# Mamba + SwiGLU layer on one core: du times B for two channel blocks per GpSimd instruction

## The chip, the cores and the metric

One core of one Trainium2 chip runs the whole program. The metric is the device time of one execution in microseconds. The kernel before takes 1815.21 us as the median of three runs (1815.02 to 1816.69).

## The reference, cut to what matters

Four sequences of 2048 tokens with 256 features go through a Mamba block, a layer norm, a SwiGLU feed-forward block with integer weights, and a second layer norm. The part that matters here:

```python
x_in, res = jnp.split(x @ W_in, 2, axis=-1)
x_conv = silu(_causal_dw_conv(x_in, conv_w, conv_b))          # u, 512 channels
dt, Bm, Cm = jnp.split(x_conv @ W_x, [DT_RANK, DT_RANK + N_STATE], axis=-1)
delta = softplus(dt @ W_dt + b_dt)
# per token, for 16 states of each channel
h = exp(delta * A) * h + delta * Bm * x_conv
y = einsum('bdn,bn->bd', h, Cm)
out = (y + x_conv * D) * silu(res) @ W_out
# feed-forward, weights are int32 times 1/127
h2 = silu(x1 @ wg.T) * (x1 @ wu.T);  out2 = h2 @ wd.T
```

## The kernel before, in words

The 8192 tokens are cut into 16 chunks of 512. Channels lie on the 128 partitions in four blocks (m = 0 to 3). One step of the program handles one chunk, in 64 beats: beat = 4n + m is state n of channel block m. In each beat

- ScalarE makes the exponential exp(delta times A) of the block (`exp`, L1104), normally into one of two PSUM banks, so that it waits for the scan two beats back;
- GpSimd makes du times B (`times_b`, L1247): du is delta times u of the block, B one row of the input spread over all partitions (`brep`). The result goes into one of DBU = 4 buffers in SBUF, so that the product of beat b waits for the scan of beat b - 4;
- VectorE scans along the 512 tokens (`scan`, L1429): it takes the exponential and the product, and writes h.

Then TensorE turns the states of each n so that tokens lie on partitions (`turn`, L747). The tokens of the upper half are weighted by C on ScalarE (`weigh`, L1113, tile gt) and turned back and summed by TensorE (`turn_back`, L772). Those of the lower half are summed on VectorE (`sum_states`, L1442, tile acc). State n is first turned at beat 4n + 4, and its weights and sums come at beats 4n + 5 and 4n + 7.

Everything else is threaded into the same beats by hand: the tables `FILL_AT` (the beat of each TensorE job of the next chunk's front and the last chunk's back: projections, convolution, feed-forward), `READ_AT` (when ScalarE or VectorE read the result) and `BEAT` (all other work). Each engine's queue is in program order: a wait holds up whatever is behind it.

Silu needs another activation table on ScalarE than exp. Two sessions in a step hold it, from beat 31 to 32.5 (silu of the next chunk's u and of this chunk's z) and from 43.5 to 45 (silu of the gate; in step 0, of z). Before a session's table load ScalarE makes the exponentials of the next AHEAD = 2 beats (32, 33 and 44, 45) into the SBUF tile `da_ahead`; the exponential of the beat behind them (34, 46) follows the table load that ends the session (L1189). Scans 32, 33, 44 and 45 so read both inputs from SBUF. `HOLD = (0, 3)` makes the product of beat 47 wait until scan 45 has ended.

GpSimd's other work: delta and du of the next chunk (`positive_part`, L1279, at beats 52, 55, 60, 63; `times_u`, L1286, at 53, 56, 63, 63), y times silu(z) (`times_z`, L1298, at 8, 11, 13, 17), the normalisation (L1271) and, in step 0 from beat 13, nine instructions that turn the integer weights into floats (`cast`, L1256, L1260).

In step 0 the first delta and du are VectorE's: `first_u(m)` (L1500 for delta, L1504 for du). Its place in the queue of VectorE is one beat ahead of need:

```python
for beat in range(NH):
    if first and beat + 1 < DB:
        first_u(beat + 1)
    scan(i, beat)
```

so the order is first_u(0), first_u(1), scan 0, first_u(2), scan 1, first_u(3), scan 2, scan 3. The tap buffer `xs` (128 partitions, 4 rows of 512) is filled by DMA from beat 56.5 on for the convolution of the chunk after next and last read by TensorE at beat 26.

Of the kernel before, what the change touches and what calls it, by code (L numbers as in the profile page):

```python
# [65 lines left out]
BEAT = {"soft exp": [48.5, 51, 56.5, 56.5], "soft ln": [49, 51.5, 57, 59.5], "add u": [52, 55, 60, 63],  # L66
        "times u": [53, 56, 63, 63], "x1 cut": [29, 35], "x1 low": [30.5, 31.5], "y upper": [5.5, 6.5],
        "times z": [8, 11, 13, 17], "mean": [21, 64], "rstd": [22, 79], "shift": [24, 90],
        "square": [(21, 21, 21, 21), (64, 65, 67, 76)], "norm": [(25, 26, 26, 26), (94, 100, 104, 104)],
        "halo": -23.5, "silu uz": [31, 32.5], "silu gate": [43.5, 45]}  # L70
# [81 lines left out]
def mamba_swiglu(nc, x, x_t, w_in, conv_w, conv_b, w_x, w_dt, b_dt, a_log, d_skip, w_out, w_gate_t, w_up_t,  # L152
# [31 lines left out]
    with ExitStack() as ctx:  # L184
# [153 lines left out]
        def ahead(beat):  # L338

            for start in SILUS:  # L340
                if start < beat <= start + AHEAD:
                    return beat - start - 1
            return None

# [176 lines left out]
        def _(pe):  # L521

            def taken(c, name):

                kind, n = name.rstrip("0123456789"), int(name[-1]) if name[-1].isdigit() else 0
                return {"xin": (xin_ready, c * (DB + 1) + n + 2), "conv": (conv_raw, c * DB + n + 1),
                        "res": (res_raw, (c - 1) * DB + n + 1), "dtb": (xd_ready, 2 * c + 2), "ct": (ct_ready, c + 1),
                        "dt": (dt_abs, c * DB + n + 1), "yt": (lower_copied, c * DP + n + 1),
                        "o": (res1_done, c * TT + n + 1), "x1t": (low_ready, c * KK + n + 1),
                        "gate": (gate_raw, c * HB + n + 1), "up": (hid_ready, c * HB + n + 1),  # L530
                        "down": (res2_done, (c + 1) * TT + n + 1), "first": (first_res_raw, n + 1)}[kind]


            held_before, last_in = {}, {}
            for i in range(NCH):
                for beat in range(NH):
                    for name in FILLS:
                        begun = [("first%d" % FIRST_RES.index(name), 0, FILL_AT[name])] if i == 0 and name in FIRST_RES else []
                        if name in F_FILLS:
                            begun += [(name, c, [at + NH * (c - i - 1) for at in fill_at(c, name)])  # L540
                                      for c in (i + 1, i + 2) if c < NCH]
                        elif i > 0:
                            begun.append((name, i - 1, FILL_AT[name]))
# [1053 lines left out]
```

## Time and profile before

| | |
|---|---|
| median of three runs | 1815.21 us |
| profiled execution, its own time | 1816.19 us |
| its span in the profile | 1814.4 us |
| granted TensorE clock, mean | 0.994 |
| TensorE matmul busy | 1688.8 us (93%) |
| VectorE busy | 1687.7 us (93%) |
| ScalarE busy | 1610.2 us (89%) |
| GpSimd busy | 1589.4 us (88%) |
| chain that ended last | TensorE 68%, ScalarE 20%, GpSimd 5%, issue 4%, VectorE 2% |

The span is the time from the first to the last instruction of the program; 1.8 us of the profiled execution's time lie around it, and its time is 1.0 us above the median. The starts of the 16 steps (scan of beat 0) lie 108.1 to 108.8 us apart. "Beat" below counts within a step; times are from the start of the span.

### The profile page before, as it was taken

To read this page: it belongs to the slowest core of one execution; us is meant where nothing else is said; L and a number is where in the kernel's file an instruction comes from. 1 tells how busy PE (TensorE), PEld (TensorE's weight loads), DVE (VectorE), ACT (ScalarE), POOL (GpSimd) and SP (SyncE) were. 2 spreads that over 40 slices of the span, in tenths; PEclk is the share of its full clock that TensorE was granted. 3 is DMA by queue.
4 is the path that set the end of the run, shared out by engine and by line. 5 is a ranking of instruction groups with operands and counts; after the bars stand their busy time and mean duration, and the time that the engine had idled before them with its cause. 6 is when DMAs were issued, how large, how long until landed. Compare 5 with 4: busy or idle time off the path is not lost.

```text
span 1814.4 us, 32052 instructions
## 1 busy us (share of the span) xinstructions
PE 1688.8 (93%) x10128; PEld 1267.4 (70%) x10128; DVE 1687.7 (93%) x1957; ACT 1610.2 (89%) x2769; POOL 1589.4 (88%) x1373
## 2 busy tenths in 40 slices
PE   8879899999999999899999999999899999998788
PEld 3556676776767677676776867677676776767677
DVE  4999999999999999999999999999999999999994
ACT  4898989899899998989899898998989899898874
POOL 2989799898989989899898989989899898989960
PEclk9999999999999999999999999999999999999999
DMA  7323123222222323223232222323223232221110
GB/s 242 117 71 117 48 83 117 71 108 80 105 83 82 109 91 117 71 82 117 71 116 72 105 89 77 116 85 115 71 82 117 71 117 71 106 84 46 40 42 25
DMA packets 82104, 164.53 MB, mean 91 GB/s; under 512 B 10369, under 2 KB 28033, under 8 KB 81938
## 3 DMA queue, kind: packets, MB, share of 16 engines
q1 hardware_dynamic: 80498, 160.90, 25.3%
q8 instruction: 85, 1.39, 0.3%
q10 hardware_dynamic: 1440, 1.58, 0.3%
q14 instruction: 81, 0.66, 0.1%
HBM read 87.47 MB, written 8.91 MB: 53 GB/s over the span
## 4 chain that ended last, share of the span: by engine, by line
PE 68%; ACT 20%; POOL 5%; issue 4%; DVE 2%; DMA 0%; DVEq 0%; SPq 0%; ACTq 0%; POOLq 0%
PE ht_upper L747 10%; PE ht_lower L747 10%; PE y_upper L772 9%; PE fill L569 8%; PE fill L683 8%; PE fill L673 6%; PE fill L652 5%; POOL dbu L1247 4%; PE fill L584 3%; ACT gt L1113 3%; ACT da L1104 3%; ACT L1189 2%; ACT L1177 2%; ACT da_ahead L1104 2%; PE fill L622 2%
## 5 line engine op out<-in xcount | busy, mean ns | idle before, releaser
L1247 POOL TENSOR_TENSOR dbu<-du,brep 128x512 f32<-128x512 f32 x1024 | 1296.4, 1298 | 157.0 <-DVE h L1429 132.2
L1429 DVE TENSOR_TENSOR_SCAN h<-da,h,dbu 128x512 f32<-128x512 f32 x720 | 888.8, 1269 | 35.4 <-ACT da L1104 32.9
L1104 ACT ACTIVATE da<-delta,a_s 128x512 f32<-128x512 f32 x960 | 659.9, 694 | 58.6 <-DVE h L1429 55.1
L1113 ACT ACTIVATE gt<-ht_upper,ct 128x512 f32<-128x512 f32 x512 | 351.1, 686 | 74.1 <-PE ht_upper L747 69.5
L747 PE MATMUL ht_upper<-ident,h 128*128 128x128 f32 x2048 | 314.1, 276 | 71.2 <-ACT gt L1113 53.5
L747 PEld LDWEIGHTS ht_upper<-ident,h 128*128 128x128 f32 x2048 | 242.9, 142 | 196.6 <-issue 126.8
L1442 DVE SCALAR_TENSOR_TENSOR acc<-ht_lower,ct,acc 128x512 f32<-128x512 f32 x480 | 350.7, 731 | 7.5 <-PE ht_lower L747 6.1
L747 PE MATMUL ht_lower<-ident,h 128*128 128x128 f32 x2048 | 313.1, 276 | 23.6 <-DVE acc L1442 19.7
L747 PEld LDWEIGHTS ht_lower<-ident,h 128*128 128x128 f32 x2048 | 240.2, 142 | 99.5 <-DVE h L1429 48.3
L772 PE MATMUL y_upper<-ident,gt 128*128 128x128 f32 x2048 | 308.7, 273 | 0.0
L1429 DVE TENSOR_TENSOR_SCAN h<-da,dbu 128x512 f32<-128x512 f32 x240 | 282.5, 1209 | 18.8 <-ACT da L1104 18.0
L772 PEld LDWEIGHTS y_upper<-ident,gt 128*128 128x128 f32 x2048 | 245.7, 142 | 43.4 <-issue 30.8
L569 PE MATMUL fill<-xt_s,win_s 128*128 128x512 f32 x456 | 224.6, 595 | 9.7 <-DVE x1t L1360 9.7
L683 PE MATMUL fill<-wd_s,kb 128*128 128x256 f32 x720 | 177.7, 380 | 0.0
L683 PEld LDWEIGHTS fill<-wd_s,kb 128*128 128x128 f32 x720 | 127.3, 190 | 17.8 <-issue 6.2
L652 PE MATMUL fill<-wout_s,kb 128*128 128x256 f32 x480 | 117.5, 383 | 0.3 <-ACT kb L930 0.3
L673 PE MATMUL fill<-x1t,wu_s 128*128 128x512 f32 x360 | 110.8, 428 | 1.5 <-DVE kb L1349 1.5
L673 PE MATMUL fill<-x1t,wg_s 128*128 128x512 f32 x360 | 107.3, 420 | 0.0
L569 PEld LDWEIGHTS fill<-xt_s,win_s 128*128 128x128 f32 x456 | 75.6, 190 | 43.3 <-issue 41.3
L652 PEld LDWEIGHTS fill<-wout_s,kb 128*128 128x128 f32 x480 | 84.9, 190 | 21.2 <-POOL kb L1298 10.9
L1298 POOL TENSOR_TENSOR kb<-kb,z 128x512 f32<-128x512 f32 x60 | 77.7, 1295 | 0.0
L1279 POOL TENSOR_TENSOR delta<-delta,du 128x512 f32<-128x512 f32 x60 | 76.7, 1278 | 0.2
(188 smaller groups left out, 1892.5 us busy)
## 6 DMA issues: line engine op xcount, KB each, us to landing
brep<-b_rows SPq DMA_DIRECT2D x127, 512.0 KB, 3.7
xs<-xin SPq DMA_DIRECT2D x242, 256.0 KB, 2.5
xr<-x SPq DMA_DIRECT2D x16, 512.0 KB, 3.9
xt_s<-x_t SPq DMA_DIRECT2D x15, 512.0 KB, 3.8
out<-xr SPq DMA_DIRECT2D x15, 512.0 KB, 2.8
win_s<-w_in SPq DMA_DIRECT2D x2, 512.0 KB, 5.3
h<-xin SPq DMA_DIRECT2D x4, 256.0 KB, 4.1
h<-xin ACTq DMA_DIRECT2D x4, 256.0 KB, 4.6
```

What stands on the lines that cost most here:

```text
L569: mm = nc.tensor.matmul(front_bank(c, name)[:, :], win_s[:, k, m * P:(m + 1) * P], xt_place(c)[:, k, :], start=(k == 0), stop=(k == KK - 1))
L652: mm = nc.tensor.matmul(fill_bank(name)[:, 0:DM], kb[:, m, t * P:(t + 1) * P], wout_s[:, m, :], start=(m == 0), stop=(m == DB - 1))
L673: mm = nc.tensor.matmul(fill_bank(name)[:, :], w[:, k, n * P:(n + 1) * P], x1t[:, half, k, :], start=(k == 0 and half == 0), stop=(k == KK ...
L683: mm = nc.tensor.matmul(fill_bank(name)[:, 0:DM], kb[:, n, t * P:(t + 1) * P], wd_s[:, n, :], start=(n == 0), stop=(n == HB - 1))
L747: mm = nc.tensor.transpose(bank[:, m * P:(m + 1) * P], h_times(i, n, m, t * P, (t + 1) * P), ident[:, :])
L772: mm = nc.tensor.matmul(y_upper[m // 2][:, (m % 2) * HALF + k * P:(m % 2) * HALF + (k + 1) * P], lhsT=gt[:, (n * UPPER + k) % GT, m * P:(m ...
L1104: nc.scalar.activation(dst[:, :], delta[:, par, m, :], ACT.Exp, scale=a_s[:, m, n:n + 1])\
L1113: nc.scalar.activation(gt[:, (n * UPPER + k) % GT, :], ht_upper[:, :], ACT.Copy, scale=ct[:, par, k, n:n + 1])\
L1247: nc.gpsimd.tensor_tensor(dbu[:, beat % DBU, :], du[:, par, m, :], brep[:, n // PIECE % 2, n % PIECE, :], ALU.mult).then_inc(dbu_ready, 1)
L1298: nc.gpsimd.tensor_tensor(kb[:, blocks, times], kb[:, blocks, times], z[:, par, blocks, times], ALU.mult)\
L1429: nc.vector.tensor_tensor_scan(h_times(i, n, m, 0, T), da[beat % 2][:, :] if slot is None else da_ahead[:, slot, :], dbu[:, beat % DBU, :] ...
L1442: nc.vector.scalar_tensor_tensor(out=acc[:, par, k, :], in0=ht_lower[:, :], scalar=ct[:, par, UPPER + k, n:n + 1], in1=acc[:, par, k, :], ...
```

## The change

GpSimd's product takes two channel blocks (beats b and b + 1, b even) in one instruction of 128 x 1024, with B read twice through a broadcast operand; it waits for both blocks' du and for the scans that free both buffers, and counts up by two when it ends. There are six product buffers. `da_ahead` is gone: the exponentials ahead (beats 32, 33, 44, 45) go to two rows of the tap buffer `xs`, with the waits which that needs on ScalarE and on the DMA queue of SyncE. Silu of z is two instructions of two blocks each, both at beat 32.5, in step 0 too. The nine weight casts are ScalarE's, at beats 12, 13, 14, 15, 18, 19, 36, 38, 40 of step 0. The tables `FILL_AT`, `BANK`, `READ_AT`, `EARLY_FILL` and `EARLY_READ` are written in another layout with the same values.

```diff
-CAST_AT, WEIGHT_PARTS = 13, 9
+CAST_AT = (12, 13, 14, 15, 18, 19, 36, 38, 40)
+WEIGHT_PARTS = len(CAST_AT)
-AHEAD = 2
-DBU = 4
+AHEAD = (('xs0', 'xs1'), ('xs0', 'xs1'))
+DBU = 6
 HOLD = (0, 3)
-        da_ahead = sb("da_ahead", [P, AHEAD, T])
...
             def shift_xin(c, m):
+                if m == 0 and c > 1 and LAST_XS is not None:
+                    sp.wait_ge(h_ready, (c - 2) * NH + LAST_XS + 1)
...
-            def silu_z(c, par):
-                act.wait_ge(res_raw, c * DB)
-                nc.scalar.activation(z[:, par, :, :], z[:, par, :, :], ACT.Silu).then_inc(z_ready, 1)
+            def silu_z(c, par, half):
+                blocks = slice(half * DP, (half + 1) * DP)
+                if c:
+                    act.wait_ge(res_raw, (c - 1) * DB + (half + 1) * DP)
+                else:
+                    act.wait_ge(first_res_raw, (half + 1) * DP)
+                nc.scalar.activation(z[:, par, blocks, :], z[:, par, blocks, :], ACT.Silu).then_inc(z_ready, 1)
...
+            def cast(n, k):
+                if n < 2:
+                    third = slice(k * (HID // 3), (k + 1) * (HID // 3))
+                    copy((wg_s, wu_s)[n][:, :, third], integers(n)[:, :, third].bitcast(I32)).then_inc(w_ready, 1)
+                else:
+                    third = slice(2 * k, 2 * k + 2)
+                    nc.scalar.activation(wd_s[:, third, :], wd_s[:, third, :].bitcast(I32), ACT.Copy, scale=W_SCALE)\
+                        .then_inc(w_ready, 1)
...
             def times_b(i, par, beat):
                 n, m = beat // DB, beat % DB
                 if n == 0:
-                    pool.wait_ge(du_ready, i * DB + m + 1)
+                    pool.wait_ge(du_ready, i * DB + m + 2)
...
-                used = beat - DBU if beat >= DBU else max(b for b in range(NH) if b % DBU == beat) - NH
-                after(pool, h_ready, i * NH + max(used, HELD.get(beat, used)) + 1)
-                nc.gpsimd.tensor_tensor(dbu[:, beat % DBU, :], du[:, par, m, :],
-                                        brep[:, n // PIECE % 2, n % PIECE, :], ALU.mult).then_inc(dbu_ready, 1)
+                for b in (beat, beat + 1):
+                    used = b - DBU if b >= DBU else max(other for other in range(NH) if other % DBU == b % DBU) - NH
+                    after(pool, h_ready, i * NH + max(used, HELD.get(b, used)) + 1)
+                nc.gpsimd.tensor_tensor(dbu[:, beat % DBU:beat % DBU + 2, :], du[:, par, m:m + 2, :],
+                                        brep[:, n // PIECE % 2, n % PIECE:n % PIECE + 1, :].broadcast_to([P, 2, T]),
+                                        ALU.mult).then_inc(dbu_ready, 2)
...
                 for beat in range(NH):
-                    times_b(i, par, beat)
+                    if beat % 2 == 0:
+                        times_b(i, par, beat)
```

With `HELD` = {47: 45}, the product of beats 46 and 47 waits for scan 45.

## Rows read from the trace of the kernel before

**Rows 1.** Busy time by engine, step 0 and step 8: stretch, us, busy of each engine
```profile
34.00:143.00 109.00, 85.77 (x483) 56.41 (x483) 97.67 (x97) 91.68 (x145) 98.29 (x82) 0.95 0.28 99
903.00:1012.00 109.00, 104.31 (x630) 78.45 (x630) 102.64 (x120) 100.74 (x176) 100.33 (x87) 1.00 0.27 93
```

**Rows 2.** Who waited for whom, whole span: us in total, times, longest
```profile
DVE h L1429 <- POOL dbu L1247: 0.3, 1, 0.3
```

**Rows 3.** Chain that ended last, step 8, silu of z: start, us, what
```profile
955.60 1.80 ACT z L998
```

**Rows 4.** Instruction groups: durations in ns (min/median/max, or mean behind the busy time)
```profile
L1247 POOL TENSOR_TENSOR dbu<-du,brep x1024: 1254/1282/2175, 32.1 to 1764.4; 128x512 f32<-128x512 f32 x171
...
L1266 POOL TENSOR_TENSOR stats<-stats 128x4 f32<-128x4 f32 x30 | 6.2, 205 | 23.9 <-ACT stats L1024 23.9
...
L1003 ACT ACTIVATE kb<-kb 128x1536 f32<-128x1536 f32 x30 | 44.4, 1482 | 0.2
...
L998 ACT ACTIVATE z<-z 128x2048 f32<-128x2048 f32 x16 | 30.6, 1914 | 0.0
```

**Rows 5.** Timeline, start of step 0, VectorE and GpSimd: start, us, what [idle before]
```profile
30.67 0.69 DVE L1504 TENSOR_TENSOR du<-delta,u 128x512 f32<-128x512 f32 x1
...
32.59 1.34 DVE L1504 TENSOR_TENSOR du<-delta,u 128x512 f32<-128x512 f32 x1
33.86 1.21 DVE L1429 TENSOR_TENSOR_SCAN h<-da,dbu 128x512 f32<-128x512 f32 x1
...
36.29 1.21 DVE L1429 TENSOR_TENSOR_SCAN h<-da,dbu 128x512 f32<-128x512 f32 x1
...
40.26 2.45 DVE L1429 TENSOR_TENSOR_SCAN h<-da,dbu 128x512 f32<-128x512 f32 x2 [0.31 <-POOL dbu L1247]
...
38.89 9.87 POOL L1247 TENSOR_TENSOR dbu<-du,brep 128x512 f32<-128x512 f32 x8 [1.17 <-DVE du L1504]
```

**Rows 6.** Chain that ended last, step 0, first turn of state 0
```profile
41.68 0.97 PE ht_upper L747 x4
```

**Rows 7.** Busy time by engine around it; the clock behind the last count
```profile
38.00:42.00 4.00, 4.00 (x6) 1.54 (x7) 3.66 (x5) 1.95 (x4) 3.11 (x3) 0.50 0.71 264
```

**Rows 8.** Timeline, step 8, scans 31 to 35, and GpSimd's products 31 to 35
```profile
951.38 1.21 DVE L1429 TENSOR_TENSOR_SCAN h<-da,dbu 128x512 f32<-128x512 f32 x1
...
953.76 3.24 DVE L1429 TENSOR_TENSOR_SCAN h<-da_ahead,dbu 128x512 f32<-128x512 f32 x2
...
959.44 2.41 DVE L1429 TENSOR_TENSOR_SCAN h<-da,dbu 128x512 f32<-128x512 f32 x2 [1.80 <-ACT da L1104]
...
948.60 6.19 POOL L1247 TENSOR_TENSOR dbu<-du,brep 128x512 f32<-128x512 f32 x5
```

**Rows 9.** Timeline, step 0, scans 32 to 34, products 32 to 35, exponential 34
```profile
86.69 5.23 DVE L1429 TENSOR_TENSOR_SCAN h<-da_ahead,dbu 128x512 f32<-128x512 f32 x2
...
92.48 1.21 DVE L1429 TENSOR_TENSOR_SCAN h<-da,dbu 128x512 f32<-128x512 f32 x1
...
84.74 4.99 POOL L1247 TENSOR_TENSOR dbu<-du,brep 128x512 f32<-128x512 f32 x4
...
90.60 0.69 ACT L1104 ACTIVATE da<-delta,a_s 128x512 f32<-128x512 f32 x1
```

**Rows 10.** Timeline, steps 0, 8: products from beat 47, scans of beats 46 and 64
```profile
109.32 6.34 POOL L1247 TENSOR_TENSOR dbu<-du,brep 128x512 f32<-128x512 f32 x5 [2.74 <-DVE h L1429]
...
111.86 2.41 DVE L1429 TENSOR_TENSOR_SCAN h<-da,dbu 128x512 f32<-128x512 f32 x2 [1.97 <-ACT da L1104]
...
142.66 2.51 DVE L1429 TENSOR_TENSOR_SCAN h<-da,h,dbu 128x512 f32<-128x512 f32 x2 [1.76 <-issue]
...
977.00 3.80 POOL L1247 TENSOR_TENSOR dbu<-du,brep 128x512 f32<-128x512 f32 x3 [2.79 <-DVE h L1429]
...
980.46 2.41 DVE L1429 TENSOR_TENSOR_SCAN h<-da,dbu 128x512 f32<-128x512 f32 x2
...
1011.61 2.45 DVE L1429 TENSOR_TENSOR_SCAN h<-da,h,dbu 128x512 f32<-128x512 f32 x2
```

More of the change, by code:

```diff
@@ L23 @@
 SILU_SET = "silu_and_others"
-FILL_AT = {"xin2": (2, 2), "xin3": (5, 7), "yt0": (6,), "yt1": (9,), "conv0": (10,), "o0": (10, 10, 13, 13),
[8 rows of a table removed]
+FILL_AT = {'xin2': (2, 2),
+ 'xin3': (5, 7),
+ 'yt0': (6,),
+ 'yt1': (9,),
+ 'conv0': (10,),
+ 'o0': (10, 10, 13, 13),
+ 'o1': (13, 13, 14, 14),
+ 'conv1': (14,),
+ 'o2': (17, 17, 17, 18),
+ 'o3': (18, 18, 18, 18),
+ 'conv2': (19,),
+ 'res0': (20, 20),
+ 'res1': (23, 24),
+ 'x1t0': (26,),
+ 'conv3': (26,),
+ 'x1t1': (28,),
+ 'res2': (31, 31),
+ 'gate0': (32, 35),
+ 'res3': (32, 33),
+ 'gate1': (35, 35),
+ 'gate2': (36, 37),
+ 'gate3': (38, 38),
+ 'gate4': (38, 38),
+ 'gate5': (39, 39),
+ 'up0': (40, 44),
+ 'dtb': (42, 42, 43, 43),
+ 'up1': (45, 45),
+ 'up2': (45, 45),
+ 'dt0': (45,),
+ 'ct': (45,),
+ 'up3': (47, 47),
+ 'up4': (48, 48),
+ 'dt1': (49,),
+ 'up5': (49, 49),
+ 'dt2': (50,),
+ 'dt3': (51,),
+ 'down0': (53, 53, 53, 53, 53, 54),
+ 'xin0': (-9, -9),
+ 'down1': (55, 56, 57, 57, 58, 58),
+ 'down2': (57, 59, 59, 59, 59, 60),
+ 'down3': (62, 62, 62, 62, 62, 62),
+ 'xin1': (-1, 0)}
 FILLS = list(FILL_AT)
 FRONT = ("xin", "conv", "res", "dtb", "ct", "dt")
-BANK = {"xin2": 1, "xin3": 0, "yt0": 1, "yt1": 1, "conv0": 0, "o0": 1, "o1": 0, "conv1": 1, "o2": 1, "o3": 0,
[4 rows of a table removed]
+BANK = {'xin2': 1,
+ 'xin3': 0,
+ 'yt0': 1,
+ 'yt1': 1,
+ 'conv0': 0,
+ 'o0': 1,
+ 'o1': 0,
+ 'conv1': 1,
+ 'o2': 1,
+ 'o3': 0,
+ 'conv2': 0,
+ 'res0': 1,
+ 'res1': 0,
+ 'x1t0': 1,
+ 'conv3': 0,
+ 'x1t1': 0,
+ 'res2': 1,
+ 'gate0': 0,
+ 'res3': 1,
+ 'gate1': 1,
+ 'gate2': 0,
+ 'gate3': 1,
+ 'gate4': 0,
+ 'gate5': 1,
+ 'up0': 1,
+ 'dtb': 0,
+ 'up1': 0,
+ 'up2': 1,
+ 'dt0': 0,
+ 'ct': 1,
+ 'up3': 1,
+ 'up4': 0,
+ 'dt1': 1,
+ 'up5': 0,
+ 'dt2': 1,
+ 'dt3': 0,
+ 'down0': 1,
+ 'xin0': 0,
+ 'down1': 1,
+ 'down2': 0,
+ 'down3': 1,
+ 'xin1': 0}
 F_FILLS = sorted((name for name in FILLS if name.rstrip("0123456789") in FRONT), key=lambda name: FILL_AT[name][-1])
@@ L57 @@
 GT = 4
-READ_AT = {"xin0": -6.5, "conv0": 13.5, "res0": 25, "xin1": 2, "conv1": 16, "res1": 26, "xin2": 4.5, "conv2": 23,
[5 rows of a table removed]
[L66 to L70, printed above, removed]
+READ_AT = {'xin0': -6.5,
+ 'conv0': 13.5,
+ 'res0': 25,
+ 'xin1': 2,
+ 'conv1': 16,
+ 'res1': 26,
+ 'xin2': 4.5,
+ 'conv2': 23,
+ 'res2': 32.5,
+ 'xin3': 9,
+ 'conv3': 28.5,
+ 'res3': 35,
+ 'dtb': 45,
+ 'ct': 47,
+ 'dt0': 48.5,
+ 'dt1': 50.5,
+ 'dt2': 52,
+ 'dt3': 54,
+ 'yt0': 8,
+ 'yt1': 10,
+ 'o0': 13.5,
+ 'o1': 14.5,
+ 'o2': 19,
+ 'o3': 19,
+ 'x1t0': 27.5,
+ 'x1t1': 29.5,
+ 'gate0': 36,
+ 'up0': 45.5,
+ 'gate1': 37,
+ 'up1': 45.5,
+ 'gate2': 38.5,
+ 'up2': 45.5,
+ 'gate3': 39.5,
+ 'up3': 48,
+ 'gate4': 40,
+ 'up4': 48,
+ 'gate5': 41,
+ 'up5': 50,
+ 'down0': 54,
+ 'down1': 59.5,
+ 'down2': 61.5,
+ 'down3': 63}
+BEAT = {'soft exp': [48.5, 51, 56.5, 56.5],
+ 'soft ln': [49, 51.5, 57, 59.5],
+ 'add u': [52, 55, 60, 63],
+ 'times u': [53, 56, 63, 63],
+ 'x1 cut': [29, 35],
+ 'x1 low': [30.5, 31.5],
+ 'y upper': [5.5, 6.5],
+ 'times z': [8, 11, 13, 17],
+ 'mean': [21, 64],
+ 'rstd': [22, 79],
+ 'shift': [24, 90],
+ 'square': [(21, 21, 21, 21), (64, 65, 67, 76)],
+ 'norm': [(25, 26, 26, 26), (94, 100, 104, 104)],
+ 'halo': -23.5,
+ 'silu a': [31, 32.5],
+ 'silu b': [43.5, 45],
+ 'silu at': [31, 32.5, 32.5, 43.5, 45]}
 FIRST_FILLS = ["xin0", "xin1", "xin2", "xin3", "conv2", "conv0", "conv1", "conv3", "dtb", "dt0", "dt1", "ct", "dt2", "dt3"]
@@ L336, in filled, with taken @@
             return signal, (c - (kind == "res")) * len(order) + order.index(name) + 1
[L338 to L343, printed above, removed]
+        def taken(c, name):
+            kind, n = name.rstrip("0123456789"), int(name[-1]) if name[-1].isdigit() else 0
+            return {"xin": (xin_ready, c * (DB + 1) + n + 2), "conv": (conv_raw, c * DB + n + 1),
+                    "res": (res_raw, (c - 1) * DB + n + 1), "dtb": (xd_ready, 2 * c + 2), "ct": (ct_ready, c + 1),
+                    "dt": (dt_abs, c * DB + n + 1), "yt": (lower_copied, c * DP + n + 1),
+                    "o": (res1_done, c * TT + n + 1), "x1t": (low_ready, c * KK + n + 1),
+                    "gate": (gate_raw, c * HB + n + 1), "up": (hid_ready, c * HB + n + 1),
+                    "down": (res2_done, (c + 1) * TT + n + 1), "first": (first_res_raw, n + 1),
+                    "da": (h_ready, c + 1)}[kind]
@@ L521, in _ @@
         def _(pe):
[L523 to L543, printed above, removed]
-                        for fill_name, c, beats in begun:
-                            if beats[0] == beat:
-                                place = BANK[name]
-                                held_before[c, fill_name] = last_in.get(place)
-                                last_in[place] = c, fill_name
             def wait_bank(c, name):
@@ L1194, in step @@
                 for beat in range(NH):
-                    if ahead(beat) is None and beat not in AFTER_SILU and not (first and beat < 2):
+                    if beat not in PLACES and beat not in AFTER_SILU and not (first and beat < 2):
                         exp(i, par, beat)
```

133 lines of the change are left out of this document (81 added, 52 removed), and 17 rows, old and new, of tables (BANK, FILL_AT, READ_AT).

## The prediction

> **What bounds the kernel now.** I read three things: busy time by step, then who waits for whom, then the chain that ended last. In a middle step all four engines are busy for 100 to 104 of 109 us [rows 1], so a busy share decides nothing. The waits say more: VectorE waited for GpSimd's product once, for 0.3 us [rows 2]. In the chain of a middle step TensorE runs without a break but for the first silu session, where ScalarE leads: silu of z, table load, exponential, weight, and only then the next turn of TensorE [rows 3]. So a middle step is TensorE's time plus ScalarE's session. GpSimd is hidden there. In step 0 it is otherwise: TensorE has 86 us of work in 109, VectorE and GpSimd 98 each [rows 1]. All that starts the pipeline lies there, and step 0 is the place to look at.
>
> **Price of a pair.** A product of 512 takes 1.28 us (median), the same operation on 4 elements 0.205 [rows 4]; that is 2.12 ns an element and 2.37 us for 1024. Eight in a row took 9.87 us [rows 5], that is (9.87 - 1.28) / 7 = 1.23 from start to start, 0.05 less than one lasts. So a pair takes 2.32 us of GpSimd's time if the fixed part is saved, 2.46 (two spacings) if it is not. I take 2.33, since one slope fits both rows. GpSimd saves some 32 x 0.13 = 4 us of work a step. As nobody waits for it, that brings nothing in a middle step.
>
> **Are the products still in time?** The tight place is the end of a step. In step 8 product 47 starts at 977.00, when scan 45 ends. Now the pair 46/47 starts there, because of the hold. Up to the pair of the next beats 0 and 1 GpSimd has ten pairs and eight delta and du operations of 1.23: 33.1 us (34.4 at 2.46), with no gate that closes in between, as six buffers let it run. It ends at 1010.1 to 1011.4, and scan 0 is at 1011.61 [rows 10]. In time, by 0.2 us at worst. Scan 46 is no trouble in a middle step: the pair is done at 979.3 to 979.5, and the scan comes at 980.46 [rows 10].
>
> **Start of step 0: +3.9 us.** Here the pair waits for two du, and VectorE makes them one beat ahead. Product 0 ran beside du(1), which took 1.34 us for that instead of 0.69 [rows 5]. Now du(1) ends at 32.59 + 0.69 = 33.28, the pair runs from 33.36 to 35.7, and scan 0 starts at 35.75 instead of 33.86. Scan 1 follows by the old spacing, 2.43 later, at 38.2. Behind it stands first_u(3), done after one more spacing, at 40.7. Only then may pair 2/3 start, and scan 2, next in VectorE's queue, waits for all of it, till 43.1; what is queued behind it waits too. Scan 3 follows at 44.3 instead of 40.26, and ends 4.0 later than before. TensorE's first turn began at 41.68, right behind scan 3's old end at 41.5 [rows 5, 6], and waits till 45.6: +3.9. Bounds: 3.0, if the pair were 0.5 shorter, and 4.4.
>
> **Clock of TensorE: +1.0.** Around 38 to 42 us the granted clock is 0.50, that is 1.2 GHz, after TensorE had idled for about 4 us [rows 7]. The new wait is another 3.9 us. The old stretch at half rate reached 2 us beyond the turn and cost 1 us; if the clock stays down for 4 to 5 us of the new work it costs 2.4. I take 1.0 more, bounds 0 and 2.4.
>
> From there the chain goes through TensorE's queue, nearly closed up to beat 20, and then through VectorE, so I let both terms through whole.
>
> **First session of step 0: +0.8.** Scans 32 and 33 take both inputs from SBUF, and then VectorE and GpSimd shut each other out: the two scans took 5.23 us, as the first waited for product 35 to end [rows 9]. It lost 2.9 us. With six buffers the pair 36/37 may start when scan 31 ends (one sum of VectorE, 0.6 us, before 86.69) and lasts till 88.5; the scan waits for it and ends at 89.6, not 90.8. That relief of 1.2 us would be worth having, but silu of z now stands in the first silu session of step 0 too: 1.91 us and 0.1 for the split (below) put exponential 34 from 90.60 to 92.5, and scan 34 from 92.48 to 93.2 or 93.3 [rows 9]. So +0.8, bounds 0.6 and 1.2. In the second session ScalarE gets the 1.9 us back, but scan 46 now waits for the held pair: 109.32 + 2.33 = 111.65, about where it was, 111.86 [rows 10].
>
> **End of step 0: -0.3.** Before, GpSimd led here: scan 0 of step 1 started at 142.66, after 1.76 us of idling. Ten pairs and eight others from 109.32 give 142.5 [rows 10] (143.8 at 2.46). Take -0.3; bounds -0.3 and +1.1.
>
> **Silu of z in two: +1.5.** 2048 elements take 1.914 us and 1536 take 1.482 [rows 4]: 0.84 ns an element, 0.19 fixed. A half takes 1.05, and since 1.91 us of it are 1.80 in the chain [rows 3], each further instruction costs about 0.1. It stands on the chain in the 15 steps after step 0. Bounds 0.05 and 0.2 each.
>
> **At nothing.** Casts: nine copies of 512 elements, by the same fit 0.62 us each, 5.6 in all; ScalarE idles 17 us of step 0 [rows 1], mostly waiting for TensorE and the scans at beats 12 to 40; if that cover went, up to 5.6. On GpSimd they are gone from a place where VectorE was full. Exponentials in `xs`: the same SBUF writes; the wait for conv3 (filled at beat 26, read at 28.5) is over by beat 31, and SyncE's wait for scan 45 is over by 56.5, where the tap DMA is issued, with stores and B loads behind it. Six buffers: no time of their own.
>
> **The port in the middle steps: 0.** Scan 32 starts at 953.76 and ended 2.1 us later. Scan 31 ends at 952.59; the pair 36/37 runs from then or from the end of 34/35 (952.5 to 953.3) to 955.0 or 955.8, so scan 33 ends at 957.3 to 958.0, and the sum behind it is done by 958.7. Scan 34 comes at 959.44, on ScalarE's time, after 1.80 us of idling [rows 8]: covered. In step 0 the waiting scan let products 34 and 35 pass, though they started after it [rows 9]; if the normalisation behind 36/37 passes too, 0.5 more, still covered. The Trainium skill (SBUF — State Buffer, Who interferes with whom) says that whoever issues first has the shared pair for the whole instruction and the other blocks. By that rule the scan of step 0 would have waited only for product 33; the trace disagrees. By the rule the middle steps end at 958.7, by the row at 959.2, and the sum is the same.
>
> **Sum.** 3.9 + 1.0 + 0.8 - 0.3 + 1.5 = +6.9. The profiled execution took 1816.2 (span 1814.4 and 1.8 around it), 1.0 above the median; 1823.1 against it, **1822.1** as a median. Its bounds: 3.0 + 0 + 0.6 - 0.3 + 0.8 = 4.1 and 4.4 + 2.4 + 1.2 + 1.1 + 3 = 12.1, so 1819.3 to 1827.3. A measurement can tell some 0.2%, 3.6 us, from no change, so slower begins at 1818.8 and faster below 1811.6.
>
> **Rivals.**
> - *The port is not covered* (0.13). The block doubles with the instruction. If scan 34 comes later than ScalarE's exponential by 0.5 to 1 us in 15 steps, +7.5 to 15 on top: 1830 to 1837. For it: only 0.2 to 0.7 us are left over. Against: the idle 1.80 us.
> - *The broadcast operand costs* (0.05). A pair of 2.6 us overruns the margin at scan 0 by some 0.7 us in each step (from six pairs between beats 54 and 0, and nine before): +11, so 1833.
> - *The late start is absorbed* (0.15). VectorE and ScalarE have small gaps between beats 4 and 20; if TensorE catches up there, both first terms go: 1817.2, no change by the measurement. Against: TensorE's queue is nearly closed there.
> - *Faster: GpSimd does pace* (0.09). The chain puts 5% of the span on GpSimd, 90 us, in step 0, at the end of step 14 and in step 15, where the scans and the products wait for each other in a ring. If those are its pace, the pairs save 0.13 in 2.46 of that, 4.8 us; with the 1.2 us of scan 32, the start absorbed and z at +0.8, -5.2: 1810.0. It decides wherever a scan waits for a product. Against: only 0.3 us of such waits [rows 2].
>
> **Numbers.** Forecast 0.58. Slower 0.58 + 0.13 + 0.05 = 0.76, same 0.15, faster 0.09. The range 1816.5 to 1831 takes in the forecast, the absorbed start and the lower edge of the port rival, and leaves out the faster case, the broadcast case and the rest of the port's.
>
> **What would show it.** Scan 2 of step 0 at 43.1 and TensorE's first turn at about 45.6; the clock at 0.50 once more behind it; product instructions of 2.37 us; scan 34 of step 0 at the exponential's end; step 1 starting about 5.4 us later than 142.66, at 148.1; the other steps 108.8, each 0.1 longer. Steps of 109.2 or more would speak for the port or the broadcast, steps under 108.6 for a GpSimd that paces. Step 1 starting before 145 would be the absorbed start.

## The result and the profile after

The changed kernel takes **1822.81 us** as the median of five runs (1822.15 to 1824.02), the kernel before 1815.21: a ratio of 1.0041, 95% interval 1.003 to 1.0052. It is slower by 0.4%: by 7.6 us in the medians and by 5.96 in the two profiled executions (1822.15 against 1816.19).

The page of the changed kernel, its span, busy time and the shares of the chain that ended last:

```profile
span 1820.3 us, 32112 instructions
...
PE 1691.9 (93%) x10128; PEld 1267.5 (70%) x10128; DVE 1695.2 (93%) x1957; ACT 1616.0 (89%) x2794; POOL 1517.8 (83%) x852
...
PE 71%; ACT 19%; issue 5%; DVE 4%; POOL 2%; DMA 0%; DVEq 0%; ACTq 0%; POOLq 0%; SPq 0%
```

GpSimd, at 88% before, is at 83%, and its share of the chain went from 5% to 2%: the work was saved, and the time did not follow. Who waited for whom in the changed kernel, total us, times, longest:

```profile
POOL dbu L1403 <- DVE h L1571: 174.8, 82, 7.0
...
POOL dbu L1403 <- DVE du L1645: 26.3, 2, 21.1
...
DVE h L1571 <- POOL dbu L1403: 5.2, 2, 2.6
```

Two waits of 2.6 us stand where 0.3 stood [rows 2]. Both lie at the start of step 0. VectorE there, then GpSimd (start, us, what, idle before); they answer to [rows 5]:

```profile
32.43 0.69 DVE L1645 TENSOR_TENSOR du<-delta,u 128x512 f32<-128x512 f32 x1
35.72 1.22 DVE L1571 TENSOR_TENSOR_SCAN h<-da,dbu 128x512 f32<-128x512 f32 x1 [2.59 <-POOL dbu L1403]
...
40.00 0.69 DVE L1645 TENSOR_TENSOR du<-delta,u 128x512 f32<-128x512 f32 x1
43.28 4.64 DVE L1571 TENSOR_TENSOR_SCAN h<-da,dbu 128x512 f32<-128x512 f32 x4 [2.59 <-POOL dbu L1403]
```

```profile
33.26 2.35 POOL L1403 TENSOR_TENSOR dbu<-du,brep 128x1024 f32<-128x1024 f32 x1 [21.05 <-DVE du L1645]
40.84 6.95 POOL L1403 TENSOR_TENSOR dbu<-du,brep 128x1024 f32<-128x1024 f32 x3 [5.22 <-DVE du L1645]
```

Pair 2/3 can start only when du(3) has ended, at 40.69, and starts at 40.84; scan 3 starts at 44.42 in place of 40.26. TensorE's first turn follows, and the clock stays at 0.50, 1.2 GHz, to 50 us, where it had been back at 1.00 by 43.7 before. The second fence is busy time by stretch: us, then PE, PE's loads, VectorE, ScalarE, GpSimd, the granted clock, DMA share and GB/s:

```profile
45.67 1.11 PE L881 MATMUL ht_upper<-ident,h 128*128 128x128 f32 x4 [4.15 <-DVE h L1571]
```

```profile
46.00:50.00 4.00, 4.00 (x17) 1.94 (x16) 1.92 (x2) 2.15 (x4) 4.00 (x2) 0.50 0.00 0
```

By beat 8 the scan is 5.19 us later than before (54.08 against 48.89). In the first silu session of step 0 z's two halves and the table load stand ahead of exponential 34, and scan 34 waits for that; they answer to [rows 9]:

```profile
94.37 2.00 ACT L1136 ACTIVATE z<-z 128x1024 f32<-128x1024 f32 x2
96.39 1.28 ACT L1344 ACT_TABLE_LOAD   x1
97.68 0.69 ACT L1258 ACTIVATE da<-delta,a_s 128x512 f32<-128x512 f32 x1
```

```profile
91.65 4.17 DVE L1571 TENSOR_TENSOR_SCAN h<-xs,dbu 128x512 f32<-128x512 f32 x2
...
98.41 1.23 DVE L1571 TENSOR_TENSOR_SCAN h<-da,dbu 128x512 f32<-128x512 f32 x1 [1.72 <-ACT da L1258]
```

Scan 34 is 5.93 us late. Step 1 starts at 148.76, 6.10 late. From there to the start of step 15 the changed kernel takes 1521.91 us and the one before 1520.58: 1.34 more in 14 steps, 0.096 each. And from the start of step 15 to the end it takes 149.7 in place of 151.2: 1.5 less, which nothing in the forecast said. So 6.10 + 1.34 - 1.5 = 5.9, the difference of the two profiled executions.

### The profile page after: what moved, and what is told of

Its sections match the earlier page's. It is cut to its first block, busy times and chain, and to the rows that moved or that the text cites. A ratio compares the mean times of both kernels' runs of the same rounds, so it can differ in the third digit from the quotient of the medians.

```text
span 1820.3 us, 32112 instructions
## 1 busy us (share of the span) xinstructions
PE 1691.9 (93%) x10128; PEld 1267.5 (70%) x10128; DVE 1695.2 (93%) x1957; ACT 1616.0 (89%) x2794; POOL 1517.8 (83%) x852
## 4 chain that ended last, share of the span: by engine, by line
PE 71%; ACT 19%; issue 5%; DVE 4%; POOL 2%; DMA 0%; DVEq 0%; ACTq 0%; POOLq 0%; SPq 0%
PE ht_upper L881 10%; PE ht_lower L881 10%; PE y_upper L906 9%; PE fill L703 8%; PE fill L817 8%; PE fill L807 6%; PE fill L786 5%; PE fill L718 3%; ACT gt L1267 3%; ACT da L1258 3%; DVE h L1571 2%; PE fill L756 2%; ACT L1334 2%; ACT L1344 2%; PE fill L739 2%
## 5 line engine op out<-in xcount | busy, mean ns | idle before, releaser
L1403 POOL TENSOR_TENSOR dbu<-du,brep 128x1024 f32<-128x1024 f32 x512 | 1205.5, 2372 | 211.2 <-DVE h L1571 174.8
L807 PE MATMUL fill<-x1t,wu_s 128*128 128x512 f32 x360 | 110.6, 427 | 1.5 <-DVE kb L1492 1.5
L1415 POOL TENSOR_SCALAR xr<-xr,stats 128x256 f32<-128x256 f32 x120 | 90.1, 760 | 1.7
```

What stands on the lines that cost most here:

```text
L807: mm = nc.tensor.matmul(fill_bank(name)[:, :], w[:, k, n * P:(n + 1) * P], x1t[:, half, k, :], start=(k == 0 and half == 0), stop=(k == KK ...
L1403: nc.gpsimd.tensor_tensor(dbu[:, beat % DBU:beat % DBU + 2, :], du[:, par, m:m + 2, :], brep[:, n // PIECE % 2, n % PIECE:n % PIECE + 1, : ...
L1415: nc.gpsimd.tensor_scalar(xr[:, par, t, :], xr[:, par, t, :], rstd[:, which, t:t + 1], nmr[:, which, t:t + 1], ALU.mult, ALU.add)\
```

## The experiments

Twelve kernels ran. Each time is a median beside its ratio to the kernel before on the same chip, with its 95% interval; the runs are from several chips, where the kernel before had medians of 1814.24 to 1815.44 us, so small differences between runs of different chips go by the ratios. "Changed" is the changed kernel (1822.81 us, 1.0041). "Period" is the time from the start of one step to the next. Where no edit is said to leave something out, all of the computation is done.

**1. The first four products single.** `first_times_b` makes the product of one block and waits for its du alone:

```diff
+                    if first and beat < DB:
+                        first_times_b(beat)
-                    if beat % 2 == 0:
+                    elif beat % 2 == 0:
                         times_b(i, par, beat)
```

> The changed kernel with the products of beats 0 to 3 of step 0 alone made one block at a time again, each behind its own du; all others stay pairs. Head theory (the pairs cost 4.2 us at the start of step 0, because scan 2's pair is queued behind a pair that waited for both du, and 1.0 us more because TensorE then works at the low clock for longer): scan 3 begins at 40.3 us in place of 44.4, step 1 at 143.6 in place of 148.8, the time is 1817.6 us (1817.0 to 1818.6; the last step may move it by 1.5 either way). Rival, port (what the pairs cost lies in the scans that wait for GpSimd's port in every step): the head comes earlier but the steps after it hold at least half of the cost, 1820 to 1822. Rival, absorbed (the later start falls into idle time of step 0 anyway): step 1 begins within 1 us of 148.8, time 1822 to 1823.

1819.12 us, 1.0022 (1.0013 to 1.003). The start is back: scan 3 at 40.32, as before the change. But scan 4, whose product is now in the first pair, comes at 42.63 in place of 41.48. GpSimd (start, us, what, idle before):

```profile
38.96 1.26 POOL L1397 TENSOR_TENSOR dbu<-du,brep 128x512 f32<-128x512 f32 x1 [1.18 <-DVE du L1653]
40.18 6.98 POOL L1409 TENSOR_TENSOR dbu<-du,brep 128x1024 f32<-128x1024 f32 x3
```

That leaves 0.85 at beat 8. Step 1 starts at 144.39, 4.4 earlier than in the changed kernel, where 5.2 was expected. In this execution 1.1 and 0.3 are lost again in steps 1 and 2 (109.85 and 109.15), the first beside a stretch at the low clock:

```profile
149.00:153.00 4.00, 3.08 (x13) 2.91 (x14) 3.87 (x4) 3.12 (x6) 4.00 (x2) 0.57 0.17 49
```

The head theory has the place right and the size 1.5 us too high: the median lies above its range (1817.0 to 1818.6). The absorbed start falls: step 1 does not start near 148.8.

**2. All products single, six buffers.**

```diff
-                    pool.wait_ge(du_ready, i * DB + m + 2)
+                    pool.wait_ge(du_ready, i * DB + m + 1)
...
-                nc.gpsimd.tensor_tensor(dbu[:, beat % DBU:beat % DBU + 2, :], du[:, par, m:m + 2, :],
+                nc.gpsimd.tensor_tensor(dbu[:, beat % DBU, :], du[:, par, m, :],
```

> The changed kernel with every product single again, each behind its own du, six buffers kept, weights on ScalarE and z in halves as changed: the pairing undone alone. Head theory: outside the head a pair costs nothing, so this is the kernel of the first run again: scan 3 at 40.3, step 1 at 143.6, steps 1 to 14 at 108.78 us each as with pairs, time 1817.6 us, within 0.7 of the first run. Port rival: faster than the first run by more than 1 us, with a step period under 108.7. Rival, pairs help (GpSimd's 68 us less busy time buys something): slower than the first run by more than 1 us.

1851.44 us, 1.0197 (1.0183 to 1.0211). The pairing undone alone makes the changed kernel 29 us slower. Of the three theories only the last had the sign (slower than run 1, by 32 us), and its reason, GpSimd's busy time, is taken up in runs 6 and 7. The chain that ended last now leads through GpSimd:

```profile
POOL 34%; PE 33%; DVE 12%; issue 11%; ACT 9%; DVEq 0%; DMA 0%; POOLq 0%; SPq 0%; ACTq 0%
```

The start is no worse than it should be (scan 3 at 40.22, step 1 at 141.4 where 143.6 was expected), but steps 2 to 14 take 110.5 to 111.5. Step 5, VectorE and then GpSimd:

```profile
633.63 7.06 DVE L1568 TENSOR_TENSOR_SCAN h<-xs,h,dbu 128x512 f32<-128x512 f32 x2
```

```profile
628.28 7.43 POOL L1402 TENSOR_TENSOR dbu<-du,brep 128x512 f32<-128x512 f32 x6
635.70 1.46 POOL L1413 TENSOR_SCALAR xr<-xr,stats 128x256 f32<-128x256 f32 x1
637.13 2.48 POOL L1402 TENSOR_TENSOR dbu<-du,brep 128x512 f32<-128x512 f32 x2
640.77 1.27 POOL L1402 TENSOR_TENSOR dbu<-du,brep 128x512 f32<-128x512 f32 x1 [1.16 <-DVE h L1568]
```

Scans 32 and 33 read only SBUF and take 7.1 us for 2.5 of work. Scan 32 starts at 633.63 in a row of six products (31 to 36). Product 35 is under way; 36 starts at 634.44, while the scan waits, and passes it. The scan is through at 636.8, and the normalisation behind the row took 1.46 in place of 0.56, as now it had to wait. Scan 33 starts at 636.7, lets two more products pass (37 and 38), and runs only when GpSimd stops at 639.61; it ends at 640.7. So here a scan that waits does not get in between two products that follow each other. With four buffers product 36 could not start before scan 32 had ended; with six it can.

**3. z whole, in the second session of step 0.**

```diff
-                nc.scalar.activation(z[:, par, blocks, :], z[:, par, blocks, :], ACT.Silu).then_inc(z_ready, 1)
+                nc.scalar.activation(z[:, par, :, :], z[:, par, :, :], ACT.Silu).then_inc(z_ready, 1)
...
-                    elif at == silu_at and what[0] == "z":
+                    elif at == silu_at and (what == "z0" and not first or what == "g0" and first):
```

> The changed kernel with silu of z as one instruction of four blocks, in step 0 in the second session, as the kernel before had it; the pairs stay. Silu theory (the half of z in the first session of step 0 delays scan 34 by 0.7 us, and the split costs 0.1 us in each step): scan 3 stays at 44.4, step 1 begins at 147.9 in place of 148.8, the step period is 108.68 to 108.71 in place of 108.78, time 1820.4 us (1819.6 to 1821.2). Rival, period by something else (casts, x times D or the six buffers make the 0.1 us): the period stays 108.78 and the time is 1821.8 to 1822.0. Rival, z free: both stay, 1822.8.

1820.68 us, 1.0033 (1.0021 to 1.0044); 2.1 under the changed kernel's median, 1.5 by the ratios, 2.4 expected. The medians alone can't tell that from nothing; the trace can. From step 1 to step 15 it takes 1520.53 us, as the kernel before (1520.58): the 0.1 of each step is the split of z and nothing else. Step 1 starts at 149.10, though, and not at 147.9. In step 0 this execution had a second stretch at 1.2 GHz, 44.5 to 51.3, and was 0.84 later at beat 8 than the changed kernel, ahead of the first instruction on which the two differ. From beat 8 to step 1 it takes 94.18 in place of 94.68: moving z gives back 0.5 there, where I had expected 0.9.

**4. Both edits.** Runs 1 and 3 together.

> Both edits at once: beats 0 to 3 of step 0 single, z whole and late as before; pairs from beat 4, six buffers, casts on ScalarE, weight of x times D as changed. Theory (the head and z are the whole difference and they add): scan 3 at 40.3, step 1 at 142.7, period 108.70, time 1815.2 us (1814.2 to 1816.2), that is the kernel before. Rival, another cost is left (six buffers, casts, pairs in the middle): 1816.5 or more, with a period over 108.75. Rival, GpSimd's saved time helps once the two costs are gone: under 1813.8, with a period under 108.65.

1814.7 us, 1.0001 (0.9992 to 1.001): the kernel before again, with pairs from beat 4, six buffers and the casts on ScalarE still in it. Step 1 starts at 142.18 and steps 1 to 14 take 1520.67. The start and z are the whole of the loss, as far as the interval can tell (some 1.7 us either way). GpSimd, busy for 1518.1 us in place of 1589.4, brings nothing that can be seen.

**5. The kernel before, with the wait alone.** Singles of 1.28 us, but each waits for both du of its pair:

```diff
-                    pool.wait_ge(du_ready, i * DB + m + 1)
+                    pool.wait_ge(du_ready, i * DB + m - m % 2 + 2)
```

> The kernel before, with one thing of the change: each product, still one block, of beats 0 to 3 of a step waits for both du of its pair. Head theory (the wait for the pair's later du is what delays the start, and a single product 1.28 us long in place of 2.37 leaves the rest): the products of beats 2 and 3 begin when du 3 is there at 40.9 us in place of being waited for singly, scan 2 begins near 42.2 in place of 38.7 and scan 3 near 43.4 in place of 40.3, step 1 begins 3 to 4 us later than the 142.7 of before, and the time is 1818.6 us (1817.5 to 1820). Rival (the cost is the double length of the instruction, not the wait): scan 3 within 0.5 us of 40.3 and the time 1815.4.

1817.71 us, 1.0012 (1.0003 to 1.0021). VectorE at the start of step 0:

```profile
34.77 1.23 DVE L1429 TENSOR_TENSOR_SCAN h<-da,dbu 128x512 f32<-128x512 f32 x1 [1.46 <-POOL dbu L1247]
...
39.05 0.69 DVE L1504 TENSOR_TENSOR du<-delta,u 128x512 f32<-128x512 f32 x1
41.19 4.89 DVE L1429 TENSOR_TENSOR_SCAN h<-da,dbu 128x512 f32<-128x512 f32 x4 [1.44 <-POOL dbu L1247]
```

Scan 3 starts at 42.41, 2.15 later than before; with pairs it was 4.16. So the wait makes 2.15 of the delay and the double length the other 2.0: 0.95 at scan 0, which stands ahead of du(3) in VectorE's queue, and 2.09 at scan 2, where the second pair's length is added. I had expected 3.1 at scan 3, which put too much on the wait; the sum of the two, in the forecast, was right. Step 1 starts at 146.17, 3.5 later than before.

**6. Single products, four buffers.** `DBU = 4` on top of the edit of run 2.

> The changed kernel with every product single, each behind its own du, and four buffers: pairs and six buffers both undone, the rest as changed. Port theory (the 32 us that single products with six buffers cost come from a row of queued products on GpSimd that keeps the port while scans 32 and 33 wait; four buffers keep that row short, as in the kernel before): scan 32 about 2.0 us and scan 33 about 1.3 us long in the middle steps, step period 108.8 us, time 1818.0 us (1816.5 to 1820). Rival, GpSimd is the bound (single products are too much work for GpSimd together with what the change left it): the period is 110 or more and the time over 1835 again.

1817.32 us, 1.001 (1.0001 to 1.0019). The period is 108.79 in most steps. In step 5 scan 32 takes 1.92 us and scan 33 1.25:

```profile
627.26 3.10 DVE L1568 TENSOR_TENSOR_SCAN h<-xs,h,dbu 128x512 f32<-128x512 f32 x2
```

GpSimd is busy for 1580 us, as in run 2, and is no bound.

**7. Single products, six buffers, product 36 held.** `HOLD = (4, 3)` on top of run 2: product 36 waits until scan 33 is done.

> Single products with six buffers once more, but the product of beat 36 is held until scan 33 is done, so that the row of queued products ends at 35. Port theory: scan 32 is 2.0 to 2.6 us long in place of 3.2 and scan 33 1.25 to 1.5 in place of 4.0, the step period goes from 110.9 back to 108.8 to 109.2, time 1819 to 1825 us. Rival, GpSimd is the bound by its busy time, which is the same here: the period stays at 110 to 111 and the time near 1851.

1816.76 us, 1.0006 (0.9997 to 1.0015): one wait takes away 35 of run 2's 36 us, more than I had expected (1819 to 1825 us). Step 5, VectorE and GpSimd:

```profile
628.49 3.12 DVE L1568 TENSOR_TENSOR_SCAN h<-xs,h,dbu 128x512 f32<-128x512 f32 x2
```

```profile
631.68 1.27 POOL L1402 TENSOR_TENSOR dbu<-du,brep 128x512 f32<-128x512 f32 x1 [2.34 <-DVE h L1568]
```

The scans take 3.1 in place of 7.1 us. The row of queued products at those two scans was the cause, and GpSimd's busy time was not.

**8. Pairs, four buffers.** `DBU = 4`.

> The changed kernel with four buffers in place of six, pairs kept. Buffer theory (a pair can begin only when both of its buffers are free, so with four buffers a pair begins after the scan one beat before its own use of 2.37 us and scans start to wait for products): DVE waits for the products in every step, the period grows by 1 to 10 us, time 1835 to 1980 us. Rival, six buffers are not needed (scans come 1.7 us apart on average and one pair in hand is enough): DVE waits for products only at the head, 1822 to 1824 us.

1869.19 us, 1.0296 (1.0282 to 1.031), inside the range of the buffer theory. Steps 1 to 14 take 110.6 to 113.0 us. GpSimd waited for scans 236 times, 284.2 us, against 82 times and 174.8:

```profile
POOL dbu L1403 <- DVE h L1571: 284.2, 236, 3.8
...
DVE h L1571 <- POOL dbu L1403: 7.1, 10, 2.6
```

The waits put down to products are small (7.1 us), but in step 5 six scans (0, 12, 14, 54, 56, 58) start within 0.1 us of the end of their pair, and in the changed kernel none does. With four buffers a pair cannot start until the scan three beats before its first beat is done, and then takes 2.4 us; the scan waits at beats where GpSimd has another 1.28 us of work queued nearby (y times z, delta, du). So four buffers are too few for the pair. That these late pairs make up the whole 46 us was not shown, and five buffers did not run.

**9. Work for TensorE in the gap of the start.** 14 transposes of the identity ahead of the first turn of step 0; their results are overwritten.

```diff
+                if i == 0 and n == 0 and k == 0:
+                    pe.wait_ge(du_ready, DB)
+                    for w in range(FILLER):
+                        nc.tensor.transpose(ht_upper[:, w % TT * P:(w % TT + 1) * P], ident[:, :], ident[:, :])
                 pe.wait_ge(h_ready, i * NH + (n + 1) * DB)
```

> The changed kernel with 14 transposes of the identity, into the bank of the first turn, put on TensorE ahead of the first turn of step 0, once du 3 is there; their results are overwritten. Clock theory (of the 5.2 us by which step 0 runs late at beat 8, 1.0 is TensorE working at 1.2 GHz until 50 us because it had idled from 41.5 to 45.7): with work in that gap the clock is back at 2.4 GHz before 47 us, beat 8 is 4.2 us later than in the kernel before in place of 5.2, and the time is 1821.8 us (1821.0 to 1822.3). Rival (the clock of the start falls differently in every execution, whatever the gap): beat 8 stays 4.9 to 6.0 us later and the time is 1822.8.

1820.45 us, 1.0033 (1.0021 to 1.0044), 2.1 under run 10 of the same chip. TensorE, the same 4 us as above:

```profile
41.30 2.83 PE L889 MATMUL ht_upper<-ident 128*128 128x128 f32 x14
45.68 0.66 PE L882 MATMUL ht_upper<-ident,h 128*128 128x128 f32 x4 [1.55 <-DVE h L1576]
```

```profile
46.00:50.00 4.00, 4.00 (x25) 1.99 (x23) 2.79 (x3) 3.49 (x6) 4.00 (x2) 1.00 0.25 93
```

The clock is back at 2.4 GHz at 43.7 us, the first four turns take 0.66 us in place of 1.11, and in the same 4 us TensorE gets 25 matmuls done in place of 17. Beat 8 is 3.20 later than in the kernel before, not 5.19: filling the idle gap is worth 2.0 us, twice what I took, and the median lies below the range that I gave (1821.0 to 1822.3). Five traces with pairs at the start and no filler (the changed kernel, runs 3, 8, 10 and 11) have beat 8 at 53.90 to 55.02 and this one at 52.09, so it is more than their spread. Beat 8 is now also 1.0 less late than scan 3 (4.16): with the clock up, part of the late start is caught up. The profiled execution keeps little of it (1822.36): it lost 1.4 us in step 1, with TensorE at the low clock from 152 to 156 us.

**10. The pair behind the session held.** `HOLD = (4, 3)` in the changed kernel: pair 36/37 waits for scan 33.

> The changed kernel with the pair of beats 36 and 37 held until scan 33 is done, in every step, so that scan 32 does not wait for a pair. Covered theory (the 1.2 us by which scan 32 waits in the middle steps lie beside exponentials that come later anyway): scan 32 takes 1.3 us in place of 2.45, the norm behind the pair 0.56 in place of 2.47, the step period stays 108.79 and the time is 1822.6 us (1821.8 to 1823.2). Port rival (the wait costs part of itself in each step): the period falls by 0.1 or more and the time is under 1821. Rival from the single products, where holding gained 35 us: GpSimd's row of queued instructions costs here too, under 1819.

1822.56 us, 1.0043 (1.003 to 1.0057). VectorE around scans 32 and 33 in step 5, the changed kernel and then this one:

```profile
634.31 3.64 DVE L1571 TENSOR_TENSOR_SCAN h<-xs,h,dbu 128x512 f32<-128x512 f32 x2
637.87 0.72 DVE L1583 SCALAR_TENSOR_TENSOR acc<-ht_lower,ct,acc 128x512 f32<-128x512 f32 x1
639.85 1.28 DVE L1571 TENSOR_TENSOR_SCAN h<-da,h,dbu 128x512 f32<-128x512 f32 x1 [1.26 <-ACT da L1258]
```

```profile
634.37 2.45 DVE L1571 TENSOR_TENSOR_SCAN h<-xs,h,dbu 128x512 f32<-128x512 f32 x2
636.74 0.75 DVE L1583 SCALAR_TENSOR_TENSOR acc<-ht_lower,ct,acc 128x512 f32<-128x512 f32 x1
639.91 1.29 DVE L1571 TENSOR_TENSOR_SCAN h<-da,h,dbu 128x512 f32<-128x512 f32 x1 [2.42 <-ACT da L1258]
```

The port's wait of 1.2 us is gone and all of it comes back as a longer wait for exponential 34 (2.42 for 1.26). Covered, as forecast, with 1.26 us to spare.

**11. The casts back on GpSimd.**

> The changed kernel with the casts of the weights back on GpSimd in step 0 at the beats of the kernel before. Theory (the casts cost ScalarE nothing that the end saw, and GpSimd has room for them): 1822.8 us (1822.0 to 1823.6), step 1 begins within 0.5 us of 148.8. Rival, the casts on ScalarE delayed step 0 (scans 35 to 40 wait for exponentials behind them): step 1 begins by 148.0 and the time is 1822.0 or less. Rival on the other side, GpSimd's queue with pairs and casts delays products in step 0: 1824 or more.

1821.9 us, 1.004 (1.0028 to 1.0053), against 1822.56 for run 10 beside it: no difference that can be told. The median is 0.1 below the range that I gave (1822.0 to 1823.6), which fits the rival by which casts on ScalarE delay step 0 (1822.0 or less), but that rival wanted step 1 by 148.0. Step 1 starts at 149.67, 0.91 later than in the changed kernel and so outside the 0.5 that I gave, but scan 8 was 0.94 later already (55.02), ahead of any cast, with TensorE at 1.2 GHz from 44.8 to 51.5. From beat 8 to step 1 the two kernels take 94.65 and 94.68, so no cost of the casts shows on either engine.

**12. Single products held, z whole.** Runs 3 and 7 together.

> Single products with six buffers, the product of beat 36 held until scan 33 is done, and z as in the kernel before: the two edits that each gained, together. Theory (they add: 1816.8 less 2.1 for z): 1814.7 us (1813.8 to 1815.6), step period 108.69, step 1 begins by 142.0, which is as fast as the kernel before or up to 0.05% faster. Rival, the single products and z interact (the exponentials of the session come sooner and meet the products): over 1816. Rival, pairs are worth something in the middle steps: slower than the kernel with the first four products single and z as before, 1814.7, by more than 1 us.

1815.5 us, 1.0005 (0.9995 to 1.0014), period 108.69; inside the expected range, though step 1 starts at 143.87 and not by 142.0: this execution had 1.2 GHz from 39 to 46, and beat 8 at 50.08. In the ratio z gains nothing over run 7 (1.0006), in the trace it gains 0.1 a step as in run 3; run 7's median and this one differ by less than either is sure of. Nothing that ran is faster than the kernel before by more than its interval. Run 4 and this one tie with it.

## Why the prediction was right

Forecast 1822.1 us, measured 1822.81; slower, with a chance of 0.76.

The sum was +6.9. Between the two profiled executions, from which it was worked out, the terms came to +4.16, +1.03, +0.74, +0.17 and +1.34, that is +7.4, less 1.5 in the last step.

- *Price of a pair*, 2.37: the 512 pairs average 2.372. The broadcast operand costs nothing, and that rival is out.
- *Start of step 0*, +3.9: +4.16 at scan 3, inside the bounds. Each time in that paragraph came within 0.2 us (scan 0 at 35.72 for 35.75, scan 2 at 43.28 for 43.1, first turn at 45.67 for 45.6). Runs 1 and 5 show the cause. One premise was off without harm: the first turn of the kernel before stood at 41.68 behind four fill jobs of TensorE itself (37.93 to 41.68), not behind scan 3.
- *Clock*, +1.0: +1.03 between the two traces, but the agreement is partly luck. Run 9 shows that filling the gap is worth 2.0, and runs 1 and 4, which issue the same instructions up to the session of step 0, are 1.8 us apart at beat 8 (scan 8 at 49.74 and 47.98), while the low clock lasts to 43.6 in one and 40.8 in the other.
- *First session*, +0.8: +0.74 at scan 34 (5.93 less 5.19), and both of its halves are there. From beat 8 to scan 34 it is 43.6 us before, 42.4 in runs 3 and 4, where z is late (the relief at scan 32, 1.2), and 44.3 in the changed kernel (z, 1.9). But eleven beats on, at scan 45, it is 59.2, 59.5 and 60.0: the relief is gone and 0.5 of z is left. That the two end at the same 0.8 was not foreseen.
- *End of step 0*, -0.3: the one term with the wrong sign (its own times, 142.5 for 142.66, gave -0.2). Step 1 is 6.10 late and scan 34 was 5.93, so +0.17. GpSimd's row, 115.43 to 148.65, was 33.2 us for the 33.1 worked out, and scan 0 followed 0.11 behind it: 33.33 from the row's start to the scan, as long as before (109.32 to 142.66 [rows 10]). The row started 6.11 late, behind a scan 45 that was 6.01 late. But the row of before had 1.1 us of waits for scans in it. Single products beside the same z and casts (runs 2, 6 and 7) take 33.4 us from scan 45 to step 1, and the changed kernel 34.7. With single products scan 0 needs product 0 alone, and the row from scan 45 up to it is 26 instructions of 1.23 us, that is 32.0. With pairs product 46 is behind the hold too and product 1 comes with product 0, and the row is 33.1. So pairs lose 1.3 us here, as at the start, and the forecast had no term for it.
- *Silu of z in two*, +1.5: 1.34 in 14 steps, and run 3 takes it away to 0.05 us.
- *Casts, port, exponentials in `xs`* at nothing: run 11 for the casts, run 10 for the port, and the port rival falls with it. No run moved the exponentials back by themselves; run 4 has them in `xs` and ties with the kernel before.
- *Six buffers* at nothing: they were costed as an edit by themselves, which they are not. With pairs four buffers cost 46 us (run 8), and with single products six cost 34 (run 2 against run 6) unless the row is held. The two edits belong together.
- *GpSimd paces*: out as a gain. Its busy time fell by 72 us, and run 4, free of the two losses, is no faster than before.
- *The last step*, -1.5, had no term. Before, VectorE waited 1.11 us for TensorE in step 15, behind a stretch at 1.2 GHz (1740 to 1743.4); scan 49 came 1.17 later by it, and the other 0.3 is open. The changed kernel's trace has no such stretch between 1730 and the last microseconds, and neither the pairs nor z explain it: run 5, the kernel before but for waits, takes 149.2 from the start of step 15. The two lines of VectorE are from the kernel before:

```profile
1743.12 1.28 DVE L1429 TENSOR_TENSOR_SCAN h<-da,h,dbu 128x512 f32<-128x512 f32 x1
...
1746.20 0.69 DVE L1349 SCALAR_TENSOR_TENSOR kb<-fill,kb 128x512 f32<-128x512 f32 x1 [1.11 <-PE fill L673]
1746.81 1.27 DVE L1429 TENSOR_TENSOR_SCAN h<-da,h,dbu 128x512 f32<-128x512 f32 x1
```

The profiled executions are 5.96 apart and the medians 7.6 because the one of before was 1.0 above its median and the changed kernel's 0.7 below its own. That 1822.1 came within 0.7 us of 1822.81 is luck to this extent: each term is right to within 0.5 us, and the clock moves a single execution by more.

On the shared pair of ports, the rule of the Trainium skill that the prediction weighed (SBUF — State Buffer, Who interferes with whom: whoever issues first has it for the whole instruction) holds here in part. In the middle steps pair 36/37 kept the ports to its end while scan 32 waited, and the scan then ran ahead of the normalisation that was issued behind it; the forecast's second guess, that the normalisation would pass, was wrong. But in step 5 the normalisation, issued at 635.67, ended only at 638.14, behind scan 33, which was issued a microsecond later (636.69) and ended at 637.95. The same happens in 11 of the 14 steps from 2 to 15; in steps 4, 8 and 12 the normalisation got in between the two scans. Two lines of GpSimd in step 5 of the changed kernel:

```profile
631.02 4.67 POOL L1403 TENSOR_TENSOR dbu<-du,brep 128x1024 f32<-128x1024 f32 x2
635.67 2.47 POOL L1415 TENSOR_SCALAR xr<-xr,stats 128x256 f32<-128x256 f32 x1
```

It does not hold between products either: in run 2 product 36 started while scan 32 waited, products 37 and 38 while scan 33 waited, and all three passed.

## What to carry to other kernels

A wider instruction waits for the last of its inputs and delivers the first of its outputs late. Its price therefore stands wherever a consumer needs only the first output: here where the pipeline fills, and where a held row of products ends. Before saving an engine's work, ask who waits for it: here 72 us of GpSimd's time were worth nothing, while one instruction too many in a ScalarE session cost 0.1 us in each step. And more buffers ahead of a shared port are not free: they let one engine queue a row of work that the other has to sit out, and a single hold at the right beat took 35 of 36 us away.

## What was not expected of the hardware

- A scan that reads only SBUF and waits for GpSimd sits out a row of back-to-back TENSOR_TENSORs (3.98 us for scan 33 in run 2, of which 1.25 is work), but scan 32 gets in before a TENSOR_SCALAR. The other way round, the waiting TENSOR_SCALAR is passed by a second scan in 11 of 14 steps of the changed kernel (2.47 us in place of 0.56). Whether the kind of instruction decides, or how closely one follows another, wasn't tried.
- TensorE's clock in step 0 falls and rises at other times from one trace to the next, and the start moves with it: beat 8 lies at 53.90 to 55.02 in the five traces with pairs at the start and no filler, and at 47.96 to 50.08 in three kernels with single products and the same instructions up to there (runs 2, 7 and 12). In the 22 executions of the kernel before beside runs 1 to 4, the three at a mean granted clock of 0.997 took 1813.28 to 1813.74 us and the four at 0.993 or less 1815.48 to 1817.29; but the fifteen between reach from 1812.57 to 1817.73, so the mean clock does not tell the time of one execution. A term of 1 us can't be judged by one execution of this kernel. What decides the moment wasn't settled.
